# Copying split keys and queries on chip, and a new order of the score passes on TensorE, in an attention and mixture-of-experts block

## The reference, cut to what matters

```python
# per batch entry b, C = 128 channels, L = 512 positions
q = proj(layernorm(x), Wq, bq); k = proj(ctx, Wk, bk); v = proj(ctx, Wv, bv)
scores = einsum('bhqd,bhkd->bhqk', q, k) / sqrt(16)
attn = softmax(scores, axis=-1)
x = x + tanh(g_xattn) * einsum('bhqk,bhkd->bhqd', attn, v)
h = rmsnorm(layernorm(x)); probs = softmax(h @ router_w); top 2 experts, weights renormalised
x = x + tanh(g_ffn) * (sum over the two experts of their gated FFN of h + shared FFN of h)
```

## Time and profile before

| | us |
|---|---|
| median of 3 runs | 1382.22 (1381.18 to 1385.08) |
| the profiled execution, whole | 1395.77 |
| its span | 1393.9 |
| span up to the first exp_scores of block 0 | 52.48 |
| turns 0 to 30 (52.48 to 863.91) | 811.43 |
| turn 31 and the experts | 530.0 |

### The profile page before, as it was taken

How to read it: one execution, slowest core, us unless ns; L and a number is a source line. 1 busy time by engine, 2 the same in 40 slices (tenths; PEclk the granted TensorE clock), 3 DMA queues, 4 the chain that set the end, 5 groups by cost and what they waited for, 6 DMA issues and landing times.

```text
span 1393.9 us, 34399 instructions
## 1 busy us (share of the span) xinstructions
PE 1291.6 (93%) x12274; PEld 681.9 (49%) x12274; DVE 976.9 (70%) x1661; ACT 873.0 (63%) x1720; POOL 860.5 (62%) x1267
## 2 busy tenths in 40 slices
PE   3899999999999899989999988899999999999997
PEld 0233333333333233333333332487788878888886
DVE  5988889999998899889999888556654323333332
ACT  2488888888887788778888877534334333334332
POOL 8657687678887787868878753541114555555553
PEclk8799999999999999999999999999999999999999
DMA  7667777767876697777878753367655888886665
GB/s 188 181 196 202 196 211 202 191 197 196 202 185 197 161 207 171 193 180 196 204 174 190 184 131 95 124 173 159 123 175 96 215 212 193 186 188 113 108 109 81
DMA packets 159586, 239.87 MB, mean 172 GB/s; under 512 B 31973, under 2 KB 65388, under 8 KB 159422
## 3 DMA queue, kind: packets, MB, share of 16 engines
q1 hardware_dynamic: 141166, 200.30, 54.9%
q0 software_dynamic: 18256, 37.38, 15.0%
HBM read 132.67 MB, written 95.49 MB: 164 GB/s over the span
## 4 chain that ended last, share of the span: by engine, by line
PE 58%; DVE 12%; issue 10%; DMA 9%; SPq 4%; POOL 3%; ACT 2%; POOLq 1%; DVEq 0%; ACTq 0%
PE m_banks L957 21%; PE bank L914 11%; PE bank L883 10%; DVE row_max L1130 8%; PE m_banks L861 7%; DMA arena<-parts_q 5%; PE bank L839 3%; PE bank L889 3%; PE bank L845 2%; SPq L457 2%; POOL xs L781 1%; PE bank L979 1%; ACT arena L1414 1%; SPq L519 1%; DMA arena<-ht_d 1%
## 5 line engine op out<-in xcount | busy, mean ns | idle before, releaser
L1130 DVE TENSOR_REDUCE row_max<-m_banks 128x2 f32<-128x1024 f32 x512 | 614.9, 1221 | 88.1 <-PE m_banks L861 79.8
L1414 ACT ACTIVATE arena<-bank 128x512 f32<-128x512 f32 x1024 | 552.1, 606 | 82.1 <-PE bank L883 80.6
L883 PE MATMUL bank<-arena 112*32 112x512 bf16 x4096 | 337.6, 384 | 5.8 <-ACT arena L1414 3.0
L914 PE MATMUL bank<-arena 128*32 128x512 f32 x2048 | 283.3, 604 | 3.0 <-ACT arena L1422 2.9
L883 PEld LDWEIGHTS bank<-arena 112*32 112x32 bf16 x4096 | 115.1, 95 | 268.3 <-ACT arena L1414 134.2
L861 PE MATMUL m_banks<-arena 48*128 48x512 bf16 x1024 | 177.7, 394 | 47.6 <-DVE row_max L1130 25.4
L793 POOL DMA_INDIRECT out<-xs,ids x71 | 112.4, 1583 | 172.7 <-ACT xs L1496 136.9
L957 PE MATMUL m_banks<-w_ring,h_hi 128*128 x568 | 183.1, 403 | 0.0
L1485 ACT ACTIVATE arena<-m_banks 128x256 f32<-128x256 f32 x103 | 39.5, 384 | 188.6 <-PE m_banks L957 188.6
L861 PEld LDWEIGHTS m_banks<-arena 48*128 48x128 bf16 x1024 | 40.1, 94 | 181.6 <-DVE row_max L1130 77.5
L671 POOL TENSOR_TENSOR arena<-arena 128x512 bf16<-128x512 f32 x62 | 72.1, 1163 | 75.8 <-ACT arena L1406 72.8
(11 more groups left out here) (182 smaller groups left out, 1997.3 us busy)
## 6 DMA issues: line engine op xcount, KB each, us to landing
arena<-parts_k SPq DMA_DIRECT2D x128, 192.0 KB
arena<-parts_q SPq DMA_DIRECT2D x128, 192.0 KB
parts_k<-arena SPq DMA_DIRECT2D x64, 256.0 KB, 5.8
parts_q<-arena SPq DMA_DIRECT2D x64, 256.0 KB, 4.5
split_d<-staged SPq DMA_DIRECT2D x30, 512.0 KB, 7.9
w_ring<-split_d SPq DMA_DIRECT2D x60, 256.0 KB, 4.0
arena<-in_w SPq DMA_DIRECT2D x36, 256.0 KB, 7.7
arena<-in_ctx SPq DMA_DIRECT2D x32, 256.0 KB, 4.1
```

Source lines behind the costliest of these rows:

```text
L883: last = nc.tensor.matmul(out[c, :], k_stack[b % 3][0:SHIFTED, h, kt * P + c.start:kt * P + c.stop], q_stack[b % 3][0:SHIFTED, h, :], star ...
L914: last = nc.tensor.matmul(pv_ps[2 * DH * j:2 * DH * (j + 1), :], v_ones[b % 3][:, kt, GROUP * g + j, :], probs[pair % 3][:, j, :], start=( ...
L1130: nc.vector.reduce_max(pair, m_ps[(STEPS * b + u) // 2 % M_PAIRS], AX_X).then_inc(s_mx, 1)
L1414: nc.scalar.activation(probs[group % 3][:, j, :], bank_of["scores", b, s], ACT.Exp, scale=float(DH) ** -0.5).then_inc(s_exp, 1)
```

## The change

1. The way through DRAM goes. `copy_parts(b, n, part)` copies a part from `parts` to the rows of the stack on chip: 10 DMAs for the keys and 8 for the queries of a block (64 or 128 KB each) in place of 12. The rows of a lane are now interleaved (`SLOTS_OF`), and a pair of heads is 2j and 2j+1 of a half in place of j and j+2.
2. SP's order: the keys' parts of block i+2 come first in turn i, the queries' after `send_values`, and `row(i+1, 0)` and the loads behind all of them. `store_reciprocals` and `load_reciprocals` move forward between them.
3. TensorE's order in a group: the second pair stands after exp_scores s+3; values come right after the first pair; projections, tokens, logits and maxima come last.
4. ACT's and DVE's slots follow the banks: `evacuate` at slots 27, 31 and 11 in place of 25, 29 and 9, the keys' high part at 29 in place of 27, `take_turned` at 15 in place of 13, `take_logits` at 19 in place of 17. The reciprocal moves from slot 16 to 12.
5. POOL adds the attention of block i-1 before it splits the keys of block i+3, in place of after.

```diff
-STORED = ((LO, MID, HI, HI), (HI, HI, MID, LO))
-HELD = ((HI, LO, MID), (HI, MID, LO))
+SLOTS_OF = (((HI, HI), (HI, MID), (MID, LO)), ((HI, LO), (MID, MID), (HI, HI)))
+COPIES = tuple(sum(2 if first == second else 4 for first, second in slots) for slots in SLOTS_OF)
-EVAC_AT = {25: (3, 0), 29: (3, 1), 9: (2, 2)}
-HIGH_AT = (27, 31)
+EVAC_AT = {27: (3, 0), 31: (3, 1), 11: (2, 2)}
+HIGH_AT = (29, 31)
-RECIP_AT = 16
+RECIP_AT = 12
...
+            def copy_parts(b, n, part):
                 if part == HI:
+                    if n == 0:
+                        if b >= 3:
+                            sp.wait_ge(s_es, STEPS * (b - 2))
+                        if b < 3:
+                            sp.wait_ge(s_blank[b], 2)
                     sp.wait_ge(s_hi, 2 * b + n + 1)
+                if part == MID:
                     sp.wait_ge(s_part, 4 * b + 2 * n + 2)
+                stack, src = (k_stack, q_stack)[n][b % 3], parts[n][part]
+                for at, (first, second) in enumerate(SLOTS_OF[n]):
+                    for base in (0, LANE):
+                        rows = stack[base + at:base + at + STACK - 2:len(SLOTS_OF[n]), :, :]
+                        if part == first == second:
+                            sp.dma_start(rows, src).then_inc(s_cp[n], DMA)
+                        else:
+                            for a in range(2):
+                                if part == (first if base == LANE * a else second):
+                                    sp.dma_start(rows[:, a:HEADS:2, :], src[a:P:2, :]).then_inc(s_cp[n], DMA)
...
             for i in TURNS:
                 if is_b(i + 2):
-                    write(i + 2, 1, HI)
+                    copy_parts(i + 2, 0, HI)
+                    copy_parts(i + 2, 0, MID)
...
@@ tensor
                 if u == 0:
-                    pe.wait_ge(s_rd[b % 3], READS * DMA * (b // 3 + 1))
+                    for kind in range(2):
+                        pe.wait_ge(s_cp[kind], COPIES[kind] * DMA * (b + 1))
...
                     if is_b(i + 1):
                         max_scores(i + 1, s)
+                    if s == 0 and is_b(i - 1):
+                        values(i - 1, STEPS // GROUP - 1)
+                    if s and is_b(i):
+                        values(i, s // GROUP - 1)
+                    if is_b(i):
+                        exp_scores(i, s + 2)
+                        exp_scores(i, s + 3)
+                    if is_b(i + 1):
                         max_scores(i + 1, s + 2)
...
@@ gpsimd
+                if is_b(i - 1):
+                    add_attention(i - 1)
                 if is_b(i + 3) and i + 3 > 0:
                     split(i + 3, 0)
-                if is_b(i - 1):
-                    add_attention(i - 1)
```

88 lines of the change are left out of this document (24 added, 64 removed).

## The result

| | before | after |
|---|---|---|
| median | 1383.65 us (1381.18 to 1388.14, 4 runs) | 1418.80 us (1414.51 to 1423.37, 4 runs) |
| the profiled execution, whole; its span | 1395.77; 1393.9 | 1417.72; 1415.8 |
| first pair of block 0 | 31.88 | 24.50 |
| first exp_scores of block 0 | 52.48 | 45.74 |
| turns 0 to 30 | 811.43 | 842.70 |

The ratio is 1.025, with a 95% interval of 1.022 to 1.028: the changed kernel is slower by 35.2 us. 1406 was forecast, and slower; the median lies just above the forecast's own range, 1394 to 1418, and inside the range of 8 in 10, 1376 to 1420. The span alone grew by 21.9 us, since the profiled execution of before was some 12 us above its median and that of after was not.

What follows compares the result with a forecast made beforehand. TensorE's sequence was taken as the bound: turns of 24.8 + 1.94 + 0.3 = 27.0 us, +22 over turns 0 to 30, +2 turn 31, -6.9 start, so 1382 + 17 + 7 = 1406 us; own range 1394 to 1418.

Steps and rivals of the forecast that it cites:

- What bounds the kernel: Turns 0 to 30: TensorE's own sequence sets the pace, busy 758.39 of 811.43 us, with few gaps.
- Part 1: TensorE's groups: visiting the pairs twice costs 0.22 us a group, 1.76 a turn; the floor becomes 24.8 us.
- Part 2: Groups s = 4 and 20: values ahead of exp_scores s+2 wait for ScalarE's copy, 1.94 us a turn where 0.62 was.
- Part 3: Other waits in a turn: most late banks and VectorE's waits go; 0.3 us stays, with 0 and 1.5 as ends.
- 27.0 for both kinds: Early turns and turns with routing both take 27.0 us, 1.9 longer than the first kind, 0.9 than the second.
- POOL's new order costs nothing: GpSimd adding attention before splitting keys costs no time: additions end by 24 us, the keys' high part comes at 26.
- Part 4: Copies on chip: the queries' waits, 16 us, go; the first pair starts at 25 us, -6.9 at the start.
- tight place: `row(i, 1)` in SP's queue, behind eight copies and two denominators; no cost taken, 1 us a turn or more if held up.
- rival 3: Eight copies ahead of `row(i, 1)` make exp_scores 16 wait by 1 us: 1437 us; chance 0.08.
- Rival 1: The waits overlap, so turns take 26.1 to 26.5 us: about 1387 us; chance 0.24.
- Rival 2: VectorE's pace bounds the long turns and the 0.11 us is a wait; turns of 25.2, 1353 us; chance 0.12.
- Rival 4: The queries still come late, SP being behind by `store_reciprocals`; the 16 us stay: 1414 us; chance 0.04.

Runs made afterwards that it cites:

- the one-shape run: The changed kernel with each pair of maxima's matmuls written as eight of 112 rows and 32 columns, the scores' shape; 1419.88 us, a single execution.
- both edits: Two runs, each on the changed kernel: GpSimd splits keys ahead of adding attention, as before (1418.29 us); the routing's exponentials at slot 30, not 26 (1419.97 us).
- the kernel with the copies alone: The changed kernel with TensorE's order and ScalarE's and VectorE's slots of before; copies, SyncE's and GpSimd's orders and reciprocal's slot stay changed; 1383.02 us, ratio 1.000.
- the kernel of 1371.25: The changed kernel with TensorE's order, ScalarE's and VectorE's slots, and GpSimd's split ahead of the additions, all as before; 1371.25 us, ratio 0.991.
- the early copy and the two edits with it: The changed kernel with the values' copy one slot earlier, GpSimd's split ahead of the additions, and the routing's exponentials at slot 30; 1383.11 us, ratio 1.002.

## Why the prediction was right, and where its steps were not

**What bounds the kernel.** Right. TensorE's sequence sets the pace; the turn grew by what TensorE's row grew by and what it waits for, with VectorE's and ScalarE's work the same.

**Part 1, the second visit: the pieces right, their share of the path too large.** 0.55, 0.32, 0.55, 0.32 and 0.88 were measured, a group of 2.62 against the 2.60 forecast, and the one-shape run shows that the 0.11 us is a cost of going over. "With nothing beside it" was wrong for the effect: alone, the visit costs 0.4 to 0.65 us a turn, and not 1.76, since it takes the place of waits for VectorE's reductions. In the changed kernel the floor of a turn, from the pieces in the timeline, is 8 x 2.62 + 0.88 x 2 + 0.90 + 0.58 + 0.31 + 0.71 = 25.2. The forecast had 24.8; the turnings of maxima take 0.39 and 0.32, where 0.2 each was taken.

**Part 2, values ahead: the mechanism right, the size somewhat too large.** The waits stand where they were put, s = 4 and s = 20, for ScalarE's copy, and are the largest of the trace. Measured as the prediction measured them, the two groups are 0.80 us over 2.62 each, 1.60 together, where 1.94 was the term. The step that was off is "from exp_scores to values that chain is 1.84": it is 1.67 in both groups (193.46 to 195.13 and 207.00 to 208.67). By the rows of ScalarE the copy ends 1.52 and 1.53 us after exp_scores start, sooner than the 1.6 at which the forecast was to fall; the turn came to 27.0 all the same. And the copy is not all of the 1.60: moved one slot earlier it gave 0.77 us back in an early turn, 19.5 us in all. The other 0.83 stayed: banks that exp_scores of the same groups get late, among them the logits' bank (0.38 us of idle time a turn, 10.9 us in 28 waits), which the change itself empties two slots later. That is why the early copy gave half of what its theory expected.

**Part 3, the other waits: about right outside these groups.** 0.3 us a turn was taken. 25.2 and 1.60 leave 0.2 us of the 27.0, nearly all of it exp_scores 0 and 1, which take 0.72 and not 0.55 (205.64 to 206.36). The late banks of s = 4 and s = 20, 0.83, are larger than the 0.1 that it allowed at s = 20. The turn of 27.0, met to 0.03, was forecast as 24.8 + 1.94 + 0.3 and is 25.2 + 1.60 + 0.2: a floor 0.4 too small against terms 0.3 and 0.1 too large. That they cancel so closely is luck.

**A term that was not there: every fourth turn.** "27.0 for both kinds" left the routing out. Turns 0 to 30 came to 842.7 us and not 834, and the longer turns (4.5, 1.0, 1.6, 1.0, 1.0 and 1.6 over 27.0, and 1.5 in those beside them) are some 12 us, against which the last turns are shorter. In the longest the rows show how: GpSimd's additions beside VectorE's routing, then ScalarE's exponentials. For the turns of 28.0 it stays open, since they outlast both edits. "POOL's new order costs nothing" is a step that failed all the same: under TensorE's old order it costs 11.8 us, by another way.

**Part 4, the copies.** The start is right: first pair at 24.50 (25 forecast), 6.7 us earlier for exp_scores (6.9). The queries' waits went, and the DMA share with them. The row of maxima, the "tight place", held in the changed kernel; rival 3 named the right wait, and it holds the copies under TensorE's old order, at a pace of 25 to 26 us a turn, but for another reason than "eight copies ahead": with the split in its old place the same eight copies stand ahead and the waits are 1.9 us in all, and moving the row ahead of four of them gave nothing more. The step that failed there is "add_attention gets its reciprocals some 20 us into the turn": in the kernel with the copies alone their transfer went out at 450.89 and GpSimd could start at 458.19, 5.70 us late, and between 130 and 860 us it waited so 19 times, 73.8 us in all. In the changed kernel it waited 3.9 us in 3 times in that stretch; that the slower turn of 27.0 hides it is argued from this, not tested.

**Turn 31** came 2.6 us shorter where +2 was forecast; which part did it was not looked into.

**The median.** The median is 12.8 us above the forecast. 1.4 are the median of before, 1382.2 then and 1383.65 beside the runs of after. 4.9 are the span: +17 was forecast and +21.9 came, from 9 us too few in the turns (+31.3 for +22, the long turns above all) and 4.6 too many in turn 31. The last 6.3 are the step from the profiled execution to the runs: 7 us were added (the text before the sum says 8, half of the queries' 16), and 13.3 came (35.2 less 21.9). Before's profiled execution stood 12.1 us above its median and that of after 1.1 below: nearly all of the excess was missing from the timed runs. An estimate of the queries' waits in them comes from the kernel of 1371.25, 12.4 us under before: 6.7 are the start, so some 6 are left for those waits, where 8 was taken. It holds only if nothing else differs, and the pairs' waits for VectorE are 10 us longer in that kernel's trace (35.7 against 25.4).

**The rivals.** Rival 1 (1387, waits overlap) is what the early copy and the two edits with it make: 1383.11 and turns of 26.3. With the late copy it did not come. Rival 2 fell, with the one-shape run against its 0.11. Rival 3's wait came in another kernel, by way of GpSimd. Rival 4 fell: no waits for the queries' copies.

## What to carry to other kernels

Before pieces of TensorE's row are moved apart, read from start to start what each piece takes behind each neighbour; then ask what each wait that goes was covering, since a cost on the busiest engine reaches the end only by what exceeds them (0.4 to 0.65 of 1.76 us here). Move a consumer forward only together with its producer's slot on the other engine: values went ahead of two exp_scores, ScalarE's copy stayed in its slot, and moving it too gave back 19.5 of the 35 us. And test a change of many parts by its halves: the copies, with one of the change's own moves put back, are 12.4 us faster than the kernel before, while the whole is 35.2 us slower.

## What the hardware showed that was not expected

- Going from matmuls of 32 columns to pairs in 128 columns and 48 rows costs TensorE about 0.11 us, and by the streams' times as much on the way back: scores take 0.55 ahead of such a pair and 0.43 to 0.45 ahead of a pair written in their own shape, and a pair with twice the streams takes 0.43 where the old one takes 0.32.
- A small tensor_tensor of VectorE took 1.32 and 1.01 us in place of 0.19 and 0.16 while a tensor_tensor of GpSimd on 128 x 512 ran beside it, and ended with it. With GpSimd's operations in another order the second one never took over 0.16 us, and the first 0.56 at most. That the two engines hold each other is an inference from where the rows stand; it was not measured alone.
- Copies on chip of 128 KB landed in a median of 2.8 us in the changed kernel, where 4.0 was the median in the kernel before, whose DMA engines were busy for 0.73 of the turns against 0.53. The load alone does not explain it: in the kernel of 1371.25 the same 256 copies took 3.7 us at a DMA share of 0.54. What else sets the time stays open.

DMA issues (count, KB each, us to landing), of the changed kernel and of that of 1371.25:

```profile
arena<-arena SPq DMA_DIRECT2D x256, 128.0 KB, 2.8
```

```profile
arena<-arena SPq DMA_DIRECT2D x256, 128.0 KB, 3.7
```
